# Causal attention in one kernel of eight layers: sums inverted in a packed layout, stacks moved within SBUF, diagonal blocks of four heads in one bank, value product copied

## The reference, cut to what matters

```python
xh = jnp.einsum('bsi,hoi->bhso', x, Wl) + bl[None, :, None, :]
Q = jnp.einsum('bhsi,hid->bhsd', xh, Wq)
K = jnp.einsum('bhsi,hid->bhsd', xh, Wk)
V = jnp.einsum('bhsi,hid->bhsd', xh, Wv)
scores = jnp.einsum('bhsd,bhtd->bhst', Q, K)
causal = jnp.triu(jnp.ones((s, s), dtype=bool), k=1)
scores = jnp.where(causal[None, None], -jnp.inf, scores)
A = jax.nn.softmax(scores, axis=-1)
F = jnp.einsum('bhst,bhtd->bhsd', A, V)
cat = jnp.transpose(F, (0, 2, 1, 3)).reshape(b, s, h * hd)
return cat @ Wo.T + bo
```

## Time and profile before

| | |
|---|---|
| median of 3 runs | 4063.19 us |
| the profiled execution | 4064.07 us |
| its span | 4062.3 us |
| TensorE busy over the span | 3463.0 us (85%) |
| VectorE, ScalarE, GpSimd | 1972.3, 1551.9, 444.0 us |
| stage 7 with its weights | about 2924 to 3622 us |
| granted TensorE clock, mean | 0.883 of full |

### The profile page before, as it was taken

The page is one execution under the profiler, slowest core; times in us unless marked ns, Lnnn a source line. Parts: engine busy times, 40 slices in busy tenths (PEclk is TensorE's granted clock), DMA queues, the critical chain, the costliest instruction groups (busy, mean ns, idle before and its releaser), DMA issues. The chain is left out here.

```text
span 4062.3 us, 51063 instructions
## 1 busy us (share of the span) xinstructions
PE 3463.0 (85%) x15954; PEld 2145.8 (53%) x15954; DVE 1972.3 (49%) x3990; ACT 1551.9 (38%) x3190; POOL 444.0 (11%) x498
## 2 busy tenths in 40 slices
PE   6499999967999899776886999999748988887998
PEld 3244444434777697433443555555435555545775
DVE  3456665643999812442243334333336666643223
ACT  2255555532444311223321444444314444432443
POOL 0000000000000000000000333333103332320000
PEclk8599999976999999887766999999859989986998
DMA  2344444421111100000002221121034434401110
GB/s 82 112 136 134 135 134 139 134 65 47 42 49 54 40 9 0 2 0 31 11 0 74 87 119 68 68 89 47 21 109 127 128 117 127 125 1 45 62 62 18
DMA packets 158169, 289.51 MB, mean 71 GB/s; under 512 B 39510, under 2 KB 113752, under 8 KB 151221
## 3 DMA queue, kind: packets, MB, share of 16 engines
q1 hardware_dynamic: 150678, 278.48, 20.7%
q10 hardware_dynamic: 7360, 9.44, 0.7%
HBM read 193.03 MB, written 94.34 MB: 71 GB/s over the span
## 5 line engine op out<-in xcount | busy, mean ns | idle before, releaser
L1171 PE MATMUL moe_o_ps<-moe_hid,moe_w 128*128 128x373 f32 x1152 | 389.9, 481 | 14.2 <-DVE moe_hid L1239 14.2
L2080 ACT ACTIVATE lstm_gate<-lstm_g_ps,lstm_w 128x373 f32<-128x373 f32 x480 | 264.5, 573 | 352.3 <-DVE lstm_state L2114 182.7
L2038 PE MATMUL lstm_g_ps<-lstm_xm,lstm_w 128*128 128x373 f32 x960 | 371.7, 484 | 8.4 <-POOL lstm_xm L1999 8.4
L398 PE MATMUL moe_h_ps<-stage_z_part,moe_wh 128*128 128x374 f32 x1152 | 339.3, 376 | 5.5 <-ACT stage_y L1186 1.7
L2556 ACT ACTIVATE caus_probsT<-caus_s_ps 128x234 f32<-128x234 f32 (+5 forms) x512 | 216.2, 438 | 299.8 <-PE caus_s_ps L2448 176.2
L2616 DVE TENSOR_REDUCE caus_nmx<-caus_a_ps 128x1 f32<-128x320 f32 (+6 forms) x512 | 235.7, 500 | 154.7 <-PE caus_a_ps L2430 133.7
L2042 PE MATMUL lstm_g_ps<-lstm_state,lstm_w 128*128 128x373 f32 x768 | 303.5, 477 | 0.0
L1171 PEld LDWEIGHTS moe_o_ps<-moe_hid,moe_w 128*128 128x128 f32 x1152 | 217.3, 191 | 127.8 <-issue 20.5
L894 DVE TENSOR_REDUCE rel_nmax<-rel_s_ps 128x1 f32<-128x746 f32 x192 | 179.2, 933 | 198.5 <-PE rel_s_ps L751 154.1
L858 ACT ACTIVATE rel_probs<-rel_s_ps,rel_nmax 128x746 f32<-128x746 f32 x192 | 170.0, 885 | 255.7 <-DVE rel_nmax L894 151.5
L1197 ACT ACTIVATE moe_ex<-moe_h_ps,moe_w 128x373 f32<-128x373 f32 x320 | 173.4, 575 | 222.8 <-PE moe_h_ps L398 221.4
(11 more groups left out here) (370 smaller groups left out, 6183.1 us busy)
## 6 DMA issues: line engine op xcount, KB each, us to landing
lstm_row<-gates SPq DMA_DIRECT2D x32, 1536.0 KB, 13.6
moe_gate<-gates SPq DMA_DIRECT2D x18, 1536.0 KB, 7.0
caus_stack<-caus_xh SPq DMA_DIRECT2D x64, 373.0 KB
caus_qs<-caus_stack SPq DMA_DIRECT2D x16, 768.0 KB, 5.7
caus_ks<-caus_stack SPq DMA_DIRECT2D x16, 768.0 KB, 8.5
caus_stack<-caus_x SPq DMA_DIRECT2D x32, 373.0 KB
moe_w<-in_moe_w SPq DMA_DIRECT2D x18, 514.0 KB, 3.6
rel_shear<-rel_probs SPq DMA_DIRECT2D x32, 256.0 KB, 2.9
```

Source lines behind the costliest of these rows:

```text
L398: mm = nc.tensor.matmul(out, w[i], x[j], start=(start and n == 0), stop=(stop and n == len(terms) - 1))
L1171: mm = nc.tensor.matmul(o_ps[i % 2][:, 0:HALF], w[s][:, HID + j * P:HID + (j + 1) * P], hid[i % 2][:, j, :], start=(j == 0), stop=(j == HJ ...
L2038: mm = nc.tensor.matmul(bank, w[e][:, g * P:(g + 1) * P], xm[x % 4][:], start=True, stop=(s == 0))
L2080: nc.scalar.activation(gate[x % 2][g][:], g_ps[n % RING][:, 0:HALF], ACT.Tanh if g == 2 else ACT.Sigmoid, bias=w[e][:, 9 * P + g:9 * P + g ...
```

## The change

Four things change in `causal_attention`, and nothing outside stage 7.

1. *Sums.* ScalarE copies the sums out of PSUM into `su` (`empty_sums`). A DMA takes one row per head (4 x 768) and lays it out as 128 x 24 (`c_in`), VectorE inverts that, a DMA stores it to DRAM, and four DMAs load it back, broadcast over the 32 rows of each head, into `r`. All of it is issued by SP at the end of its iteration, with waits between. VectorE multiplies once, over 746 columns (`normalise`).
2. *Stacks.* The DRAM tensor of the stacks is gone. 24 DMAs per turn (two sides, three parts, four heads) move 32 x 746 blocks from `x` and `xh` to the stack in SBUF. There are three stacks instead of two and one pair `x`, `xh` per side instead of two, so the copies of the next turn's projections wait for the moves.
3. *Pieces.* A diagonal block of all four heads is one piece in one bank: one matmul writes the mask for four heads (`start_with_mask`), four add the scores. Blocks beside the diagonal are packed as 4, 2 or 1 heads per bank. The mask inputs grow from 128 x 128 to 128 x 1024. There are 22 pieces per turn instead of 32; the sums stand at pieces 1 and 2, the reciprocal behind piece 9, the multiplication behind 15, the output at 18 and 20.
4. *Value product.* ScalarE copies `o_ps` to `o_sb` (`empty_values`) at the start of the next iteration; the next turn's value products wait for the copy.

```diff
+def packed(tile, c0, c1):
+    out = []
+    for at in range(c0, c1, BANK):
+        w = min(BANK, c1 - at)
+        together = next(n for n in (HPG, 2, 1) if n * w <= BANK)
+        out += [(tile, at, at + w, tuple(range(h, h + together))) for h in range(0, HPG, together)]
+    return out
...
-        V_LAG, SUM_AT, OUT_AT = 4, (2, 4), (10, 12)
+        V_LAG, SUM_AT, INVERT_AT, F_AT, OUT_AT = 4, (1, 2), 9, 15, (18, 20)
...
+                    if has(m - STACKS):
+                        sp.wait_ge(s_full, (m - STACKS + 1) * NI)
+                    for side, dst in enumerate((qs, ks)):
                         sp.wait_ge(lo_ready, m * 2 + side + 1)
-                        if side == 0 and has(m - 2):
-                            sp.wait_ge(loads1[p], m // 2 * 32)
                         order = (xh, xh, x) if side == 0 else (xh, x, xh)
                         for k in range(3):
-                            sp.dma_start(stack_d[p, side, :, k * D3:(k + 1) * D3, 0:L], order[k][p][side][:]).then_inc(stores[p], 16)
-                    sp.wait_ge(stores[p], (m // 2 + 1) * 96)
-                    if has(m - 2):
-                        sp.wait_ge(s_full, (m - 2) * NI + last_of[3] + 1)
-                    for side, dst in enumerate((qs, ks)):
-                        sp.dma_start(dst[p][0:K_S, :, 0:BANK].bitcast(F32),
-                                     stack_d[p, side, :, :, 0:BANK].rearrange("h r c -> r h c")).then_inc(loads0[p], 16)
+                            for hh in range(HPG):
+                                sp.dma_start(dst[m % STACKS][k * D3:(k + 1) * D3, hh, 0:L].bitcast(F32),
+                                             order[k][side][hh * D3:(hh + 1) * D3, :]).then_inc(moved[m % 2], 16)
+                m = n - 1
+                if has(m):
+                    ring.wait_emptied(sp, ("sum", m, 1))
+                    ring.wait_emptied(sp, ("sum", m, 0))
...
+                    sp.dma_start(c_in[:], su[0:P:D3, :].rearrange("h (s c) -> h s c", c=C)).then_inc(sums_out, 16)
+                    sp.wait_ge(inverted, m + 1)
...
+                    sp.dma_start(sums_d.rearrange("h (s c) -> (h s) c", c=C), c_out[:]).then_inc(inverse_out, 16)
+                    sp.wait_ge(inverse_out, (m + 1) * 16)
...
+                    for hh in range(HPG):
+                        sp.dma_start(r[hh * D3:(hh + 1) * D3, :], sums_d[hh, 0:L].partition_broadcast(D3)).then_inc(r_in, 16)
...
-                mm = nc.tensor.matmul(s_ps[x % 3][0:rows, 0:q1 - q0], ks[p][0:K_T, hh, j * P:k1], qs[p][0:K_T, hh, q0:q1],
-                                      start=True, stop=not diag)
+                out = heads_of(s_ps[x % 3][0:rows, :], heads, q1 - q0)
                 if diag:
-                    mm = nc.tensor.matmul(s_ps[x % 3][0:rows, 0:rows], mask[:, 0:rows], identb[:, 0:rows],
-                                          start=False, stop=True)
+                    start_with_mask(s_ps[x % 3], rows, 1)
+                for at, hh in enumerate(heads):
+                    mm = nc.tensor.matmul(out[:, at, :], ks[s][0:K_T, hh, j * P:k1], qs[s][0:K_T, hh, q0:q1],
+                                          start=not diag, stop=not diag or hh == HPG - 1)
...
+            def empty_values(n, piece):
+                c0, c1 = SPANS[piece]
+                act.wait_ge(v_done, (n + 1) * T)
+                if n > 0:
+                    act.wait_ge(f_ready, n)
+                nc.scalar.copy(o_sb[:, c0:c1], o_ps[:, c0:c1]).then_inc(o_copied, 1)
...
-                if side == 0 and half == 0 and n >= 2:
-                    act.wait_ge(stores[n % 2], n // 2 * 96)
+                if side == 0 and half == 0 and n >= 1:
+                    act.wait_ge(moved[(n - 1) % 2], ((n - 1) // 2 + 1) * 6 * HPG * 16)
...
+            def invert(n):
+                dve.wait_ge(sums_out, (n + 1) * 16)
+                if n > 0:
+                    dve.wait_ge(inverse_out, n * 16)
+                nc.vector.reciprocal(c_out[:], c_in[:]).then_inc(inverted, 1)
+
+            def normalise(n):
+                dve.wait_ge(r_in, (n + 1) * HPG * 16)
+                dve.wait_ge(o_copied, 2 * (n + 1))
```

More of the change, by code:

```diff
@@ L2414, in turn_maxima, with start_with_mask @@
                                     K["ident"][:]).then_inc(a_full, 1)
+            def start_with_mask(bank, rows, transposed):
+                nc.tensor.matmul(heads_of(bank[0:rows, :], range(HPG), rows), identb[0:rows, 0:rows],
+                                        masks[0:rows, transposed, :].rearrange("p (h c) -> p h c", h=HPG)[:, :, 0:rows],
+                                        start=True, stop=False)
             def row_scores(n, i):
[L2417 to L2418 removed]
+                t, k0, k1, heads = ROWS[i]
+                s = n % STACKS
                 if i == 0:
[L2420 to L2422 removed]
+                    pe.wait_ge(moved[n % 2], (n // 2 + 1) * 6 * HPG * 16)
                 q1 = min((t + 1) * P, L)
@@ L2697, in stage7_layout @@
         "caus_bo": f["L3_attn_bo"][:, None],
-        "causal_mask": np.where(late, -1e30, 0.0).astype(np.float32),
+        "causal_masks": np.stack([np.tile(np.where(m, -1e30, 0.0), (1, HPG)) for m in (late, late.T)], 1).astype(np.float32),
     }
```

229 lines of the change are left out of this document (114 added, 115 removed).

## The result

The changed kernel takes 4091.10 us (median of five runs, 4082.53 to 4109.29); the kernel before, on the same chip, 4064.03. The ratio is 1.0067 with a 95% interval of 1.0044 to 1.0089: 27 us slower where 75 us faster was forecast, and above the end of the forecast range (4048). The profiled execution took 4109.29 us, 45 above that of before, but 10 of these arise ahead of stage 7 (it starts that much later) and have nothing to do with the change. The stage itself grew from 697.5 to 732.9 us.

The account below looks back on a forecast made before the run. TensorE, with gaps from waits, was taken as the bound. Start -31.5, turn 0 -2, steady turns -46 and end +5 gave -74.5, so 3989 us against the median of 4063.19; range 3935 to 4048.

Parts of the forecast that it names:

- The start: Stage 7's beginning: earlier first stack and shorter wait for the maxima save 31.5 us, first row score 22 us earlier.
- turn 0: The first turn, which has no sums to process: 2 us saved.
- Part 1: Sums: TensorE's reciprocal waits go, 2.9 us a turn saved; the new chain hardly stalls VectorE, 0.3 us a turn charged.
- Rival B: Sums' chain comes late, moves issuing at 0.60 us: 3.3 us a turn lost, 4040 us; chance 0.20.
- The multiply at its own 0.94 us: VectorE's multiply behind row piece 15: taken at its old price, with no term for being held up.
- Part 3: Diagonal blocks: 32 more float32 weight loads against 36 fewer bf16 ones cost TensorE 1.5 us a turn (0 to 2.2).
- Part 2: Stacks moved within SBUF instead of through DRAM: nothing gained in steady turns, only at the start.
- Half of the clock comes back: TensorE's steady turns: of 3.8 us a turn lost to the slow clock, 1.9 return.
- rival A: TensorE's clock comes back whole: 1.9 us more a turn over 14 turns, 3962 us; chance 0.27.
- The end: After the last column scores nothing covers the sums' chain, 13 instead of 6 us to the last add: net +5 us.
- C: Moves run no faster than the old stores' transfer, deciding at 0.84 us a move: slower, 4117 us; chance 0.08.
- L2419's loads: TensorE's 128-wide float32 load and matmul pairs at this line: sign that they stay at 0.125 us a pair.

Follow-up runs that it names:

- e1: The changed kernel with GpSimd adding the exponents head by head, twelve short additions a turn for three long ones: 4036.1 us, 37.5 a turn.
- e4: The changed kernel with the 24 moves made only for the first three stacks, later turns reusing them (wrong outputs): 3954.2 us, 31.8 a turn.
- e6: The changed kernel with the product of values and inverse sums moved from VectorE to GpSimd, the sums' chain still on SP: 4037.2 us, 36.8 a turn.
- e12: The changed kernel with VectorE's multiply reading its first operand from a PSUM bank, in two instructions (output not valid): 4025.6 us, 37.2 a turn.
- e7: The changed kernel with the new sums and value product undone, moves and packed diagonals kept: 3985.7 us, ratio 0.9780 to the kernel before.
- e16: The kernel before with only the stack moves within SBUF added; diagonals, sums and value product as before: 4019.6 us, 37.0 a turn.
- e8: The changed kernel with sums, value product and stack moves undone; packed diagonals and three long GpSimd additions stay: 4063.3 us, 37.3 a turn.
- e15: e14 with the output projections one piece later, at 19 and 21 for 18 and 20: 3958.9 us, 32.3 a turn.
- e14: e9 with the last turn inverting its sums straight from their banks and multiplying from o_ps, without copies and transfers: 3969.8 us.
- e9: The changed kernel with the sums' transfers on ScalarE's queue and GpSimd's last addition waiting for the previous turn's multiply: 3983.2 us, 33.1 a turn.
- e17: e3 with GpSimd's last four additions waiting for the multiply: 3986.9 us, 34.0 a turn.
- e3: The changed kernel with both short head-by-head GpSimd additions and the sums' transfers on ScalarE's queue: 4090.3 us, 40.9 a turn.

## Why the prediction was wrong, step by step

**The start (-31.5, turn 0 -2): right, a little short.** The first column score came 72.3 us after the start of the stage for 104.1, -31.8. The first row score came 17.5 earlier and not 22. Turn 0 gave more than 2: from the first column score to the second turn's maxima it took 21.0 us for 28.9, TensorE busy all the time in both, at a clock of 1.00 for 0.73.

```profile
2987.15 0.75 PE L2447 MATMUL caus_a_ps<-caus_ks,caus_qs 96*128 96x128 f32 x4
...
3006.84 0.75 PE L2466 MATMUL caus_s_ps<-caus_qs,caus_ks 98*128 98x128 f32 x4 [0.67 <-DMA caus_qs<-caus_nmT]
```

These answer to the earlier trace rows.

**Part 1, "about no wait of VectorE, and the ring's two or three pieces cover what there is": the first step that failed.** Issue was taken as 0.45 us, "near the middle" of 0.34 and 0.60; it is 0.59, 0.63 with the gap to the next, nearly the upper bound, which was the store of this very stack. So 24 moves took over 4 us more, and the wait is 5.6 us a turn. Rival B had exactly this price (0.60) and put 3.3 us a turn on it: it credited the ring with cover that isn't there. A wait of 5.6 us cost the turn 5.7 (e1 37.5 against e4 31.8, which also has the long additions): TensorE is idle 2.8 us more, and busy 3.0 us more at the lower clock, 0.92 for 1.00.

**The multiply at its own 0.94 us: the second, and no rival had it.** It cost 43.1 - 37.5 = 5.6 us a turn (6.3 by e6, 5.9 by e12). No row of before could show it, since the multiply there read PSUM. But it could have been foreseen: the change moves an input from PSUM to SBUF beside an engine that is busy 12 us a turn, and the rule is in the section of the Trainium skill named above (SBUF — State Buffer, Who interferes with whom). The prediction took the multiply, the one instruction whose operand changed place, at its old price.

**Together** these are 43.1 - 31.8 = 11.3 us a turn, 147 us in the 13 (the ratios of the change and of e4 differ by 3.6%, or 145 us), against a forecast of 0.3 us a turn for the chain. Without them the turn is 31.8 us, shorter than the 34.3 predicted, for three further steps were wrong to the other side:

**Part 3, +1.5 us of loads a turn: wrong.** The 0.07 us a load came from the earlier trace rows, from matmuls of 128 columns in a row, and the loads of the packed pieces do stand there, but TensorE's time did not grow (e7, e16). By the Trainium skill's figure (TensorE: Matmul & The Clock Gate, Back-to-back issue gap) they would have cost 0.9 us a turn, an estimate; these runs show about none.

**Part 2, "this gives nothing there" in the steady turns: wrong once the diagonals are packed.** Moves take 2.8 us off the turn of e8 (37.3 to 34.5 in e7), and TensorE's wait for the maxima falls by 14 us over the 13 turns. (Its "each half turn" is each turn, by the order of SP's queue; no term uses it.)

**"Half of the clock comes back": nearly all did**, once neither wait was left: 1.00 in each turn of e4, 0.99 over the turns of e15, which has the moves (rival A's mechanism). With both waits it fell instead, to 0.85.

**The end, +5: +10.2.** The working had 7 us more in the chain of the last turn, and e14, without that chain, gives 6.8 back; the credit for the missing row pieces was not there, and 3.4 us are not accounted for.

**The rivals.** B and A were both true mechanisms, one hiding the other; C's condition, an issue of 0.84 us, was not met, and "slower" came without it, by two waits that each stop TensorE for the same ring. Predicted signs: "VectorE's wait for the c_in and r loads under 2 us a turn" failed for c_in (5.6) and held for r; "no wait of a row score for c_out or fT above 1 us" failed; L2419's loads held at 1.50 us for 12.

**Open:** what starts the turns at a lower clock in e9, e14 and e15. Nearly all have a longer wait for r (1.2 us and more), but two of e15 with 1.9 keep the full clock, and in e17 a turn of 36.8 at 0.85 waits no longer for VectorE than its neighbours. Open too is why e8 has turns of 37 to 39 us at 0.83 to 0.86 with short waits, and why a series of short additions holds the multiply in e3 and not in e1.

## What to carry to other kernels

When an operand moves from PSUM to SBUF, look at what GpSimd does at that place in the turn: a VectorE instruction with two SBUF inputs took 0.94 us beside an idle GpSimd, and beside a busy one it waited at least for the end of the running addition, in e3 for a whole series. Then fix the order with a wait: GpSimd's wait in e9 is 1.3 us a turn, and the race that it ends cost over 6 us of a turn and was decided by a quarter of a microsecond. Many small transfers on one queue cost their issue, here the same with 93 and 47 KB, and a short, urgent transfer belongs in front of them or on another queue; and a blocking wait on the engine that empties a small ring has to be priced in full, not less what the ring "covers".
